# A three-layer gated graph network and a graph attention layer on one core: weights prepared by the host, inputs laid out by partition, and all engine queues re-ordered

## The reference, cut to what matters

```python
h = jnp.maximum(_layernorm(x), 0.0)
A = (adj != 0)
for i in range(3):                          # layers, same GRU weights in all
    m = einsum('bnd,de->bne', h, weight[i])
    aggr = einsum('bst,bsd->btd', A, m)
    h = gru_cell(aggr, h, w_ih, w_hh, b_ih, b_hh)
x = x + h
h = jnp.maximum(_layernorm(x), 0.0) @ W.T   # W (128, 128), a (1, 256)
e = f_i[:, None] + f_j[None, :]             # f_i = h @ a1, f_j = h @ a2
att = softmax(where(adj > 0, leaky_relu(e, 0.2), -9e15))
out = x + att @ h
```

## Time and profile before

| what | value |
|---|---|
| median of 3 runs | 482.17 us (480.09 to 482.74) |
| the profiled execution | 480.5 us |
| its span in the trace | 478.7 us |
| PE busy | 451.7 us (94%) |
| DVE busy | 423.4 us (88%) |
| ACT busy | 354.0 us (74%) |
| POOL busy | 154.6 us (32%) |
| DMA, moved | 26.34 MB |
| chain that ended last | PE 86%, DVE 6%, ACT 3%, issue 3%, POOL 1%, DMA 1% |

### The profile page before, as it was taken

The page is one execution under the profiler, slowest core; times in us unless marked ns, Lnnn a source line. Parts: engine busy times, 40 slices in busy tenths (PEclk is TensorE's granted clock), DMA queues, the critical chain, the costliest instruction groups (busy, mean ns, idle before and its releaser), DMA issues.

```text
span 478.7 us, 8083 instructions
## 1 busy us (share of the span) xinstructions
PE 451.7 (94%) x2547; PEld 376.3 (79%) x2547; DVE 423.4 (88%) x1087; ACT 354.0 (74%) x641; POOL 154.6 (32%) x170
## 2 busy tenths in 40 slices
PE   4779999999999999999999999999999999998575
PEld 3557787888888888888888888888888888786565
DVE  1778987999999999999999999999999999997853
ACT  3256666787979788787879788797969788686374
POOL 2332245143332414343342424342341424132500
PEclk9889999999999999999999999999999999999979
DMA  6332000230210303030220303030120300000001
GB/s 184 124 108 80 1 23 0 90 112 22 91 43 7 128 0 112 22 112 22 61 74 1 133 1 111 23 109 25 50 82 1 134 1 2 23 1 23 24 1 44
DMA packets 26746, 26.34 MB, mean 55 GB/s; under 512 B 840, under 2 KB 18512, under 8 KB 26704
## 3 DMA queue, kind: packets, MB, share of 16 engines
q1 hardware_dynamic: 26704, 25.83, 16.5%
HBM read 21.63 MB, written 4.19 MB: 54 GB/s over the span
## 4 chain that ended last, share of the span: by engine, by line
PE 86%; DVE 6%; ACT 3%; issue 3%; POOL 1%; DMA 1%; DVEq 0%; ACTq 0%; POOLq 0%; SPq 0%
PE X L1256 18%; PE G L1374 10%; PE G L1363 5%; PE R L1240 5%; PE R L1241 5%; PE R L1242 4%; PE Z L1241 4%; PE Z L1240 4%; PE Z L1242 4%; PE G L1341 3%; PE X L1308 3%; PE HN L1240 2%; PE IN L1240 2%; PE IN L1241 2%; PE IN L1242 2%
## 5 line engine op out<-in xcount | busy, mean ns | idle before, releaser
L1256 PE MATMUL X<-A_ring,nat_hi 128*128 128x512 f32 x192 | 78.7, 410 | 2.0 <-POOL nat_lo L261 2.0
L1256 PE MATMUL X<-A_ring,nat_lo 128*128 128x512 f32 x192 | 76.6, 399 | 0.0
L1374 PE MATMUL G<-hp,probT 128*128 128x128 f32 x512 | 67.6, 276 | 0.8 <-DVE out_sb L923 0.7
L1374 PEld LDWEIGHTS G<-hp,probT 128*128 128x128 f32 x512 | 62.1, 192 | 1.7 <-issue 0.9
L911 DVE SCALAR_TENSOR_TENSOR prob<-e 128x512 f32<-128x512 f32 x64 | 44.0, 688 | 14.8 <-ACT e L464 14.8
L463 ACT ACTIVATE e<-g,nb 128x512 f32<-128x512 f32 x64 | 46.6, 728 | 13.6 <-DVE nb L904 13.4
L261 POOL TENSOR_TENSOR nat_lo<-h,nat_hi 128x512 fp32r<-128x512 f32 x16 | 20.7, 1293 | 103.6 <-DVE nat_hi L786 98.4
L270 POOL TENSOR_TENSOR hT_lo<-hT,hT_hi 128x512 fp32r<-128x512 f32 x19 | 24.6, 1295 | 80.4 <-ACT hT_hi L390 55.7
L402 ACT CAST agg_hi<-X 128x512 fp32r<-128x512 f32 x48 | 27.9, 582 | 29.7 <-PE X L1256 29.7
L464 ACT ACTIVATE e<-g,nb 128x512 f32<-128x512 f32 x64 | 45.8, 716 | 0.0
L1256 PEld LDWEIGHTS X<-A_ring,nat_hi 128*128 128x128 f32 x192 | 36.7, 191 | 11.3 <-POOL nat_lo L261 2.7
(11 more groups left out here) (136 smaller groups left out, 1208.7 us busy)
## 6 DMA issues: line engine op xcount, KB each, us to landing
adj_raw<-in_adj SPq DMA_DIRECT2D x16, 1024.0 KB, 5.6
x_ring<-in_x SPq DMA_DIRECT2D x16, 256.0 KB, 2.8
out_x<-out_sb SPq DMA_DIRECT2D x16, 256.0 KB, 2.2
wih_in<-in_L_gnn_w_ih SPq DMA_DIRECT2D x1, 192.0 KB, 3.1
wl_in<-in_L_gnn_weight SPq DMA_DIRECT2D x1, 192.0 KB, 4.1
whh_in<-in_L_gnn_w_hh SPq DMA_DIRECT2D x1, 192.0 KB, 4.1
w_in<-in_L_gnn_W SPq DMA_DIRECT2D x1, 64.0 KB
vec_in<-in_L_gnn_b_ih SPq DMA_DIRECT2D x1, 1.5 KB
```

The source lines that it names most:

```text
L1256: mm = pe.matmul(X[:], part[s][:, c], A_ring[:, (k - s) % RING, c], start=(c == 0 and part is nat_hi), stop=(c == C - 1 and part is nat_lo))
L1374: mm = pe.matmul(G2[:, c * D:(c + 1) * D], probT[:, c % 2, j], hp[:, (k + 1) % 2, j, 0:D], start=(j == 0), stop=(j == C - 1))
```

## The change

The host hands over four arrays instead of nine. `inner` holds w_ih and the three layer weights, both transposed, in 768 columns; `outer` holds w_hh transposed, W transposed, two empty columns, W, and the eight vectors as columns, 650 in all. `x`, `adj` and the output are stored as (graph, partition, chunk, column), so that one partition's part of a graph is one contiguous run of 2 KB (x, out) or 8 KB (adj). The factor 0.5 goes into `wi_high` and `wi_low`, and the factors 0.5 and 0.25 into `whh_high` and `whh_low`. All turning of weights on PE and all copies of turned weights are gone.

x and adj loads have a semaphore for even and one for odd graphs. SP issues x and adj of graph 0, then outer and inner, then x and adj of graph 1, which wait for nothing.

The low part of graph 0's features (`natural_low0(0, 0)`) goes from POOL to DVE. The lists of all engines are in another order, in the first graphs, in `full(i)` and in the last iterations.

```diff
             def load_weights():
-                sp.dma_start(wih_in[:], w_ih.rearrange("(g p) d -> p g d", p=P)).then_inc(gi_loaded, 16)
-                sp.dma_start(wl_in[:], weight.rearrange("l p e -> p l e")).then_inc(gi_loaded, 16)
...
+                sp.dma_start(outer_in[:], outer).then_inc(outer_loaded, 16)
+                sp.dma_start(inner_in[:], inner).then_inc(inner_loaded, 16)
+
+            def load_x(i, k):
+
+                if i >= RING:
+                    sp.wait_ge(x2_done, i - GA)
+                if i >= 2:
+                    sp.wait_ge(x_loaded[i % 2], i // 2 * 16)
+                sp.dma_start(x_ring[:, k], x[i]).then_inc(x_loaded[i % 2], 16)
...
+            load_x(0, 0)
+            load_adjacency(0, 0)
+            load_weights()
...
             def wi_high(l):
 
                 act.wait_ge(wi_made[l], 1)
-                act.copy(wi_hi[:, l], (G0, G1, G2)[l][:, 0:3 * D]).then_inc(wi_hi_done[l], 1)
+                act.activation(wi_hi[:, l], (G0, G1, G2)[l][:, 0:3 * D], ACT.Identity, scale=0.5).then_inc(wi_hi_done[l], 1)
...
             def whh_high():
-                dve.wait_ge(whT_done, 1)
-                dve.tensor_copy(whh_hi[:], whT[:]).then_inc(whh_hi_done, 1)
+                dve.wait_ge(outer_loaded, 16)
+                dve.tensor_scalar(whh_hi[:, 0:2 * D], whhT[:, 0:2 * D], 0.5, None, ALU.mult)
+                dve.tensor_scalar(whh_hi[:, 2 * D:], whhT[:, 2 * D:], 0.25, None, ALU.mult).then_inc(whh_hi_done, 1)
...
             def make_wi(l):
 
-                pe.wait_ge(wihT_done, 1)
-                pe.wait_ge(wlT_done, 1)
-                pe.matmul((G0, G1, G2)[l][:, 0:3 * D], wlT[:, l], wihT[:], start=True, stop=True).then_inc(wi_made[l], 1)
+                pe.wait_ge(inner_loaded, 16)
+                pe.matmul((G0, G1, G2)[l][:, 0:3 * D], wlT[:, l * D:(l + 1) * D], wihT, start=True, stop=True).then_inc(wi_made[l], 1)
```

More of the change, by code:

```diff
@@ L32, with graph_block @@
 NEG = -2.0 ** 53
[L35 to L38, removed]
+def graph_block(nc, x, adj, inner, outer, out):
+    B, _, C, D = x.shape
+    N = C * P
+    LAYERS = 3
     assert D == P and LAYERS == 3 and C == 4
@@ L231, in _ @@
-            for i in range(ITERATIONS + 1):
-                body(i, i % RING)
+                    store(i - (GB + 1))
             sp.wait_ge(stored, 16 * (B + 1))
@@ L322, in _ @@
             natural_low0(4, 0)
[L323 to L329, removed]
+            for i in range(5, 16):
                 full(i)
-            natural_low0(15, 3)
+            centre2(15, 3)
             scale2(15, 3)
-            centre2(15, 3)
             normed2(15, 3)
@@ L977, in _ @@
             wi_low(0)
-            attention_vectors()
+            x_stats(1, 1)
             biases()
             neighbours_low(0, 0, 0)
-            wi_low(1)
-            x_mean(1, 1)
-            mask(0, 0)
+            adjacency(1, 1)
+            mask(1, 1)
             reset(0, 0, 0)
             before_tanh(0, 0, 0)
+            x_mean(1, 1)
             keep(0, 0, 0)
@@ L992, in _ @@
             x_stats(2, 2)
-            mask(1, 1)
+            adjacency(2, 2)
+            mask(2, 2)
+            neighbours_low(1, 1, 1)
+            wi_low(1)
             x_mean(2, 2)
-            neighbours_low(1, 1, 1)
-            adjacency(1, 1)
             state_low(1, 1, 0)
-            wi_low(2)
             reset(1, 1, 1)
@@ L1193, in _ @@
             probabilities(18, 2, 1)
+            probabilities(18, 2, 2)
             scores(19, 3)
-            probabilities(18, 2, 2)
+            offsets(19, 3)
             probabilities(18, 2, 3)
-            offsets(19, 3)
             probabilities(19, 3, 0)
@@ L1340, in project @@
                         own = three_own[:, c * (D + 2):(c + 1) * (D + 2)] if c < C - 1 else last_own[:, 0:D + 2]
-                        mm = pe.matmul(own, h2T[:, c * P:(c + 1) * P], wT[:], start=True, stop=True)
+                        mm = pe.matmul(own, h2T[:, c * P:(c + 1) * P], wT, start=True, stop=True)
                     mm.then_inc(hp_mm, 1)
@@ L1412, in full @@
                 turn_state(i, i % RING, 2)
[L1413 to L1418 removed]
+                from_state(i, i % RING, 0, Z)
+            make_wa()
             turn_input(0, 0)
[L1420 removed]
             make_wi(0)
```

644 lines of the change are left out of this document (286 added, 358 removed).

## The result

| | before | after |
|---|---|---|
| median of 20 runs each | 482.76 us (480.09 to 485.1) | 480.87 us (478.26 to 481.69) |
| ratio, 95% interval | | 0.9951 [0.9935, 0.9968] |
| span of the profiled execution | 478.7 us | 479.0 us |
| mean granted clock of it | 0.984 | 0.978 |

What follows compares the result with a forecast made beforehand. The prediction took PE's stream of matmuls to bound the middle, leaving gains at start and tail. Terms -3.5 - 0.5 + 0.5 + 0.5 = -3.0 us from a base of 481.4 gave 478.4 us, range 474.8 to 482.6.

Steps and rivals of the forecast that it cites:

- the forecast proper: Whole kernel: the summed terms hold and the time is 476.5 to 480 us; chance 0.45.
- rival 4: Start: the weights land late, at 12.4 us, so the start brings 1.0 instead of 3.5, total 480.9; chance 0.12.
- start, up to `neighbours` of iteration 1: Start, before 29.8 us: earlier data and a faster clock end it 3.5 us earlier, 0.5 to 4.5.
- Start, the data: Start: earlier adj and inner let the first `neighbours` begin at 12.7 instead of 15.4, 2.7 us earlier.
- the 11 that was to mean late loads: Start: sign of being wrong about the loads, if make_wi starts after 11 us.
- Start, the clock: Start: PE works without a stop at 2.4 GHz, another 1.2 us; more work at half clock later, minus 0.4.
- First graphs: From 29.8 to 105 us: earlier masks free DVE and a 1.1 us wait may go, -0.5 us.
- Full iterations: Full iterations: the new order costs 0.04 us a period for about twelve periods, +0.5 us, 0 to 3.6.
- The tie at nat_lo of layer 1: Full iterations, `neighbours(i, 1)`: PE and DVE's nat_lo both arrive at +8.2 us after layer 0's last Z matmul.
- rivals 2 and 3: Full iterations: order stalls PE, 481.5, chance 0.15; DVE late at both ties, 485.1, chance 0.10.
- Tail: Behind 427 us: new order costs +0.5 us, -1.5 to +1.5; wrong if the span differs by over 1.5.
- rival 5: Start and tail: inner lands by 9.7, no half clock behind 26 us, tail gains 1.5; 475.0, chance 0.18.

Runs made afterwards that it cites:

- e6: The changed kernel with A_ring and the mask of graph 0 moved behind the natural state's first half on DVE; span 477.4 us.
- e7: The changed kernel with the copy of hT's high part of graph 3 moved behind offsets and nat_lo of graph 4; span 477.0 us.
- e5: Host-packed weights with all orders of before, and x, adj and out in their old layout; 475.85 us, ratio 0.991 to before.
- e3: The changed kernel's host arrays, layouts and early loads with all queues in the order of before; 476.83 us, ratio 0.9936 to before.
- e1: The unchanged kernel before, executed again for a second trace; span 479.0 us.
- e10: The kernel before with only the weights' tiles moved in SBUF, giving full iterations' tiles the changed kernel's addresses; 477.35 us, span 475.6.
- e12: The kernel before with only the weights' tiles moved in SBUF, run again with rounds; 477.9 us against 481.8, ratio 0.9921.
- e11: The changed kernel with three repairs: graph 0's adjacency steps later, graph 3's hT copy later, the old tail order; 475.61 us, ratio 0.99 to before.
- e8: Host's preparation with before's orders from the second graph on, and a new start on DVE and PE; 475.73 us, ratio 0.9906 to before.
- e4: The changed kernel with all queues from `neighbours(16, 0, 2)` on in the order of before; 478.11 us, ratio 0.9962 to before.

## Why the prediction was right, and where it was not

The forecast was 478.4 within 474.8 to 482.6, faster as the likeliest. The time, 480.87, lies inside, and the kernel is faster by 0.5%. It lies above the 476.5 to 480 of the forecast proper, beside the 480.9 of rival 4, whose mechanism is false. The base was too low by 1.4: the twenty runs of before have 482.76, not 481.4. And the terms did not come out as they were priced; errors of up to 3 us cancelled, so the number is right in good part by luck.

| term | forecast | between the profiled executions |
|---|---|---|
| start, up to `neighbours` of iteration 1 | -3.5 | 35.42 to 32.95: -2.5 |
| first graphs, up to the first full iteration | -0.5 | from 2.47 to 2.53 ahead: -0.1 |
| full iterations, up to `neighbours(16, 0, 2)` | +0.5 | from 2.53 to 3.20 ahead: -0.7 |
| tail | +0.5 | from 3.20 ahead to 0.3 behind: +3.5 |
| sum | -3.0 | +0.3; medians -1.9 |

The 2.2 us between the two last numbers are not located: no trace shows a typical execution of before on this chip.

**Start, the data.** The loads were underrated: adj landed at 6.15 where I took 7.5 with 6.9 as the early end, and inner 6.1 us behind its issue, at 8.3, well before 9.7. So rival 4 is false. But the chain had a step that I took as unchanged: "h are ready at 7.11 + 1.65 = 8.8". It was 8.64 + 1.65 = 10.3, since the adjacency now landed while POOL had two of its small operations to do. That made `make_wi` start at 11.25, behind the 11 that was to mean late loads, which it doesn't, and `neighbours` at 13.24 instead of 12.7. e6 got 1.75 us back by the order alone. The cover I lost without seeing it was the late landing of adj itself: before, no large DVE operation could meet the statistics of x.

The Trainium skill ("SBUF — State Buffer", "Who interferes with whom") says that DVE, in the modes that use two ports, and POOL share one pair of ports, and that the one who comes second waits for the whole of the other's instruction. The trace agrees: both POOL operations end within 0.1 us of the DVE operation beside them. In e7 one of them waited even through two DVE operations, 2.35 us. The rule speaks against this change, and I had not weighed it.

The Trainium skill's rule that 512 bytes are enough for line rate ("DMA: Bandwidth & Descriptors", "Specifications") was read in the prediction as inner landing at 12.4. It landed at 8.3, and in e5, with x in rows of 512 bytes and adj in rows of 2 KB, at 9.1. So the late end was not one of row length, and no run has the prepared weights in rows of 512 bytes. Row length counts here beyond what the rule says all the same: over the sixteen loads adj took 6.0 us from issue to landing in e5 (median) and 4.9 in e3, which differs in the layout of x, adj and out alone and has adj in rows of 8 KB.

**Start, the clock.** The matmuls of graph 0 ran 0.23 apart from the second on, as forecast. But the prediction took the fall to half clock at 16 us as the result of PE's stand before it, and that is not shown: e1, e10 and e12 have the same start with stands of 1.29, 2.54 and 1.00 us, and none fell there. So the 1.2 us is a term only against executions of before that fell, and e10 and e12 have the gain without the change.

**First graphs.** The -0.5 was eaten by the wait of 1.0 us at 88.96: DVE's `ltop`, held up by POOL, the same cause with the roles changed.

**Full iterations.** The tie at nat_lo of layer 1 did hold: the stretch from 78 to 427 shows no wait beyond that one, so rivals 2 and 3 are false. The price of the new order, 0.04 us a period, is near what e11 shows against e3, e8 and e12 (27.00 against 26.94 to 26.96, so 0.04 to 0.06). One reading was off: the earlier trace rows leaves DVE 16.9 us in 349, which is 1.3 us a period, and not the "under 1 us" of rival 2. The sign of the term was still wrong, since the tiles gave 0.11 us a period. The sentence that failed is "Order does not change how many matmuls there are, so a new order can't make the 27.06 us smaller": true for the order, but a change that drops tiles moves all others, and I had looked at order alone.

**Tail.** This is the largest miss, 3.5 us where 0.5 was priced and 1.5 was named as the sign of being wrong. My walk had `project(17)` lose 0.34 us; it lost 2.0. I wrote that hT of iteration 16's middle layer comes later, and priced the wait, but not what follows it: hT_lo by POOL another 1.26 behind hT_hi, PE idle for 0.88 and 1.34, and half clock for 6.8 us behind that. And "`scores(19)` moves behind one more `probabilities`, for which nothing waits" named the wrong side. Nothing waits for that `probabilities`, but it waits itself for its exps (2.15 us), and the scores of the last graph, which are the path to the end, stand behind it: 1.1 us against before, 0.7 against e4. e4 confirms both parts together; they were not run apart. The last 0.6 against e4 lies behind `scores`, beside the half clock that lasts until 464.5 there; what makes it was not asked.

The rivals: 2, 3 and 4 are false. The forecast held by its number, with rival 5's faster landing and a tail far outside -1.5 to +1.5. That the time comes out at -1.9 and not at zero or above rests on the tiles: without their 3.9 us (e12, on another chip) the new order and the early data would together have made the kernel slower, by this arithmetic; that kernel was not run.

## What to carry to other kernels

When a change removes or adds tiles, run the old kernel with the new places as a control, since places alone moved this one by 0.8%, and a gain that seemed to come from earlier loads was mostly there without them. Before moving a load or a large DVE operation earlier, look at what POOL does at that moment, and the other way round. In the last iterations, where the pipeline drains and little work is left to cover a wait, price a wait by what the idle time does to the clock behind it, and never put an operation that waits ahead of one that the end depends on.

## What the runs showed of the hardware

- A POOL operation on 128x4 that starts during a DVE operation of 128x2048 takes 1.1 to 1.2 us instead of 0.20 to 0.25 (e3, after); in e7's start one that began beside the first of two took 2.35 and ended with the second. A DVE operation on 128x4 beside POOL's 128x512 takes 1.27 instead of 0.16.
- Tile places in SBUF: 27.06 us a period at the old ones in three traces, 26.94 to 26.96 at the new ones with the same order of instructions. In the full iterations the GRU's matmuls of 128x512 stand 0.2346 to 0.2348 us apart on average in the one and 0.231 to 0.232 in the other (some 370 distances under 0.30 us in each trace), while those of `neighbours` stand 0.231 apart in both. So the slow ones are the products with the tiles of whh and wi. By what mechanism is open.
- The first adj, 1.05 MB, landed 2.6 to 3.0 us behind x with rows of 8 KB (after, e3, e7), and 3.4 us with rows of 2 KB and x in rows of 512 bytes (e5).
- Around or behind the stand of 2.84 us for graph 0's hT, PE fell to half clock in all 14 traces, for 3.4 us in 13 and 6.7 us in one; no order of the start avoided it.
